# A cross-attention block on one Trainium2 core: TensorE's next value rows moved behind the value sums at hand

## The reference

```python
xn = layer_norm(x, g_norm)
q = xn @ Wq
k, v = jnp.split(context @ Wkv, 2, axis=-1)
q, k, v = map(split_heads, (q, k, v))
k = jnp.concatenate([nk, k], axis=2)
v = jnp.concatenate([nv, v], axis=2)
q = l2norm(q) * q_scale
k = l2norm(k) * k_scale
attn = jax.nn.softmax(jnp.einsum('bhid,bhjd->bhij', q, k) * 8.0, axis=-1)
out = jnp.einsum('bhij,bhjd->bhid', attn, v)
out = out.transpose(0, 2, 1, 3).reshape(b, -1, INNER) @ Wout
return layer_norm(out, g_out)
```

## Time and profile before

| | |
|---|---|
| time, 3 runs | 1354.71, 1362.23, 1365.42 us; median 1362.23 |
| profiled execution | time 1356.67 us, span 1354.6 us, mean granted TensorE clock 0.89 |
| busy | PE 1159.6 us (86%), PEld 746.0, DVE 591.5, ACT 494.3, POOL 439.7 |
| chain that ended last | PE 75%, DVE 10%, issue 9%, ACT 4%, POOL 2% of the span |
| the block of the change | from the first scores at 853.4 us to the last line 1947, which starts at 1267.64 us |

### The profile page before, as it was taken

The page is one execution under the profiler, slowest core; times in us unless marked ns, Lnnn a source line. Parts: engine busy times, 40 slices in busy tenths (PEclk is TensorE's granted clock), DMA queues, the critical chain, the costliest instruction groups (busy, mean ns, idle before and its releaser), DMA issues.

```text
span 1354.6 us, 19075 instructions
## 1 busy us (share of the span) xinstructions
PE 1159.6 (86%) x8054; PEld 746.0 (55%) x8054; DVE 591.5 (44%) x1006; ACT 494.3 (36%) x687; POOL 439.7 (32%) x218
## 2 busy tenths in 40 slices
PE   7999967898787999978775896999999999999358
PEld 4645532365365545544352784677677677677234
DVE  2212357313444632345222514555655655655445
ACT  3344531333132644530332112544345445355011
POOL 0255400000000345500000000577577577577100
PEclk9899968899587999986995796999999999999669
DMA  8333300003000133320013003113113213110100
GB/s 350 140 147 139 129 0 1 0 1 125 0 1 1 74 135 134 140 109 0 0 67 136 1 1 124 64 64 125 63 64 110 79 64 113 68 71 1 68 0 8
DMA packets 23700, 98.77 MB, mean 73 GB/s; under 512 B 2752, under 2 KB 2752, under 8 KB 19904
## 3 DMA queue, kind: packets, MB, share of 16 engines
q1 hardware_dynamic: 23616, 97.56, 18.8%
HBM read 63.74 MB, written 33.82 MB: 72 GB/s over the span
## 4 chain that ended last, share of the span: by engine, by line
PE 75%; DVE 10%; issue 9%; ACT 4%; POOL 2%; DMA 0%; POOLq 0%; DVEq 0%; ACTq 0%
PE PSUM L1865 9%; PE PSUM L1906 9%; PE PSUM L1445 9%; PE PSUM L1926 8%; PE PSUM L1534 3%; PE PSUM L1471 3%; PE PSUM L1454 2%; PE PSUM L1625 2%; PE PSUM L1636 2%; PE PSUM L1489 2%; PE PSUM L1998 1%; DVE ARENA L933 1%; PE PSUM L1822 1%; PE PSUM L1590 1%; PE PSUM L1832 1%
## 5 line engine op out<-in xcount | busy, mean ns | idle before, releaser
L459 POOL TENSOR_TENSOR CK<-CK,ARENA 128x2048 f32<-128x2048 f32 x64 | 290.4, 4537 | 143.4 <-ACT ARENA L703 139.5
L1293 DVE TENSOR_TENSOR ARENA<-PSUM,RK 128x512 f32<-128x512 f32 x256 | 164.1, 683 | 114.7 <-PE PSUM L1906 114.6
L703 ACT ACTIVATE ARENA<-ARENA,WB 128x1024 f32<-128x1024 f32 x128 | 147.0, 1148 | 184.0 <-DVE ARENA L1293 183.9
L397 POOL TENSOR_TENSOR RSTD<-VE,MHALF 128x4 f32<-128x4 f32 x17 | 17.2, 1009 | 473.5 <-DVE VE L769 407.1
L1926 PEld LDWEIGHTS PSUM<-ARENA 128*64 128x64 f32 x2048 | 110.5, 137 | 48.6 <-ACT ARENA L703 43.1
L1906 PE MATMUL PSUM<-ARENA 64*128 64x128 f32 x2048 | 131.8, 278 | 2.7 <-ACT WB L698 2.2
L1445 PE MATMUL PSUM<-CT,WK 128*128 128x512 f32 x256 | 126.9, 622 | 2.4 <-ACT W L483 1.8
L1906 PEld LDWEIGHTS PSUM<-ARENA 64*128 64x128 f32 x2048 | 119.4, 188 | 14.6 <-issue 10.6
L1865 PE MATMUL PSUM<-CK,CT 128*128 128x512 f32 x256 | 126.9, 618 | 0.0
L1926 PE MATMUL PSUM<-ARENA 128*64 128x128 f32 x2048 | 125.9, 276 | 0.4 <-ACT ARENA L703 0.4
L1445 PEld LDWEIGHTS PSUM<-CT,WK 128*128 128x128 f32 x256 | 43.3, 192 | 64.0 <-issue 29.5
(11 more groups left out here) (394 smaller groups left out, 1919.7 us busy)
## 6 DMA issues: line engine op xcount, KB each, us to landing
ARENA<-kept_keys SPq DMA_DIRECT2D x16, 2048.0 KB, 8.3
kept_keys<-KEYS SPq DMA_DIRECT2D x64, 256.0 KB, 2.0
kept_keys<-W SPq DMA_DIRECT2D x64, 256.0 KB, 2.0
CT<-in_ctxT SPq DMA_DIRECT2D x4, 1024.0 KB, 9.9
CK<-in_l0f_experts SPq DMA_DIRECT2D x1, 4096.0 KB, 22.9
CK<-in_ctxk SPq DMA_DIRECT2D x1, 4096.0 KB, 12.7
ARENA<-in_l2f_experts SPq DMA_DIRECT2D x2, 2048.0 KB, 8.2
ARENA<-in_l2f_experts SPq DMA_DIRECT2D x1, 3072.0 KB, 14.0
```

The lines of the kernel that those rows point to most:

```text
L459: nc.gpsimd.tensor_tensor(LS[b % 2], LS[b % 2], PR[:, t % 2, :], ALU.add)\
L703: act(p, p, ACT.Exp, bias=SHIFT).then_inc(sem("l3x_probs"), AC.sends("l3x_probs"))
L1293: ve.tensor_tensor(PR[:, k, q * 512:(q + 1) * 512].rearrange("p (j n) -> p j n", j=4), PSUM[:, 2 + q, :].rearrange("p (j n) -> p j n", j=4 ...
```

## The change

In the loop over tiles TensorE issues the value sums of tile t, and at a batch's first tile the null values in front of them, before the value rows of tile t+1 and not behind them (and behind finish_sums). Nothing else is changed: the same instructions, the same waits, the same order on the other engines.

```diff
                 if t > 1 and t % KEY_TILES == 1:
                     finish_out(t // KEY_TILES - 1)
+                if t % KEY_TILES == 0:
+                    null_values(t // KEY_TILES)
+                values(t)
                 if more:
                     value_rows(t + 1, 0)
                     value_rows(t + 1, 1)
                 if t and t % KEY_TILES == 0:
                     finish_sums(t // KEY_TILES - 1)
-                if t % KEY_TILES == 0:
-                    null_values(t // KEY_TILES)
-                values(t)
             finish_sums(B - 1)
             finish_out(B - 1)
```

## The result

The changed kernel is slower: a median of 1404.97 us (1390.71 to 1410.2) against 1358.47 us for the kernel before, ratio 1.0351 with a 95% interval of 1.0287 to 1.0414. The forecast was 1400 us, in a range of 1376 to 1416. Runs more than 1.5% above the fastest of their kernel count as slow and are left out of the ratios, so a ratio need not be that of the medians given.

The account below looks back on a forecast made before the run. TensorE bounds the kernel between batch ends. Ordinary tiles 21.4, batch ends 17.0, start -1.9 and end +3.8 give +40.3 us: 1397.0 on the profiled scale, 1402.5 on the median's; forecast 1400, range 1376 to 1416.

Parts of the forecast that it names:

- The ordinary tile: Inside a batch: value sums wait 4.28 us after rows, cover only 3.91; tile 6.18 us against 5.797, +0.383 in 56 tiles.
- The batch end: Three batch ends: null values wait for ScalarE's copy, about 6.1 us idle before line 1947; +5.7 us each.
- Start and end: Block's start: null values and V(0) before R(1), -1.9 us; block's end: denominators 4.66 us after V(63), +3.8 us.
- the sum: Whole block: 21.4 + 17.0 - 1.9 + 3.8 = +40.3 us, giving 1397.0 us.
- two scales: Whole time: 1397.0 us from the profiled execution, 1402.5 from the median of the runs; 1400 taken.
- (a): Rival: ordinary tiles pay no wait, only the ends do; 1375.6, some 1378 us between the scales; chance 0.07.
- (c): Rival, every V(t): TensorE passes waiting value sums and starts the rows behind; time stays 1357 to 1362 us; chance 0.05.
- (b): Rival: short pauses in tiles bring the clock down; 1423 us with a tenth of tiles slow, 1530 with half; chance 0.07.
- the stretch of an earlier block: Evidence for no clock loss in tiles: idle in small pieces, 30.84 us busy of 34.00, granted clock 1.00.
- TensorE's busy share inside a batch: Sign inside a batch: TensorE busy for some 94% at a granted clock of 1.00.

Follow-up runs that it names:

- copies-last kernel: Changed kernel, with VectorE copying the first value rows behind quarters 2 and 3, ScalarE the second behind the second exponential: median 1371.36 us, ratio 1.0123.
- the extra copy: One more 128 x 512 VectorE copy per tile before the first value rows' copy: block 491.26 us on the changed kernel, 404.88 on the kernel before.
- The run with 128 rows: Changed kernel with the null-value matmuls over 128 rows of weights in place of one: block 445.76 us, 6.2 less.

## Why the prediction was right, point by point

**The ordinary tile** was right: 6.186 us measured for 6.18, 4.29 us from rows to values for 4.28, and by the measured 0.389 us a tile 56 of them are 21.8 us for 21.4. That it is the copies' place and nothing of TensorE's own is shown by the copies-last kernel (back to 5.797) and the extra copy (+0.6 us a tile after, 0 before). The one row that carried it was the end of the block, where the wait could be seen without cover.

**The batch end** was right in its steps and too small in its size: +7.5 us each in place of +5.7. The null values came 7.09 us after V(15), as worked out; the idle ahead of line 1947 was 6.03 us for 6.1. The missing part is the clock: at the three ends V(16), V(32), V(48) took 3.34, 3.17 and 3.07 us for 1.90, and from R to line 1937 it was 2.94, 3.07 and 3.22 for 2.71, 5.0 us in all. The run with 128 rows takes this part away, and a little of line 1947 with it, and comes out at 445.8, 41.5 over the kernel before, near the forecast's 40.3. Of the remaining 2.4 us most is at line 1947 and the values behind it, where the lower level lasted longer than forecast: line 1947 takes 3.69 us to the next (a granted 0.50) for 3.5, and V(17) to V(18) is 6.59, 6.70 and 6.73 us for 6.18.

**Start and end** were right: V(0) 1.9 us earlier (860.16), 10.84 us from V(62) to line 1937, as in the sum:

```profile
1294.60 1.97 PE L1926 MATMUL PSUM<-ARENA 128*64 128x128 f32 x32
1296.50 1.98 PE L1865 MATMUL PSUM<-CK,CT 128*128 128x512 f32 x4
1300.78 1.97 PE L1926 MATMUL PSUM<-ARENA 128*64 128x128 f32 x32 [2.30 <-ACT ARENA L703]
1305.44 1.94 PE L1937 MATMUL PSUM<-CK,WA 128*64 128x512 f32 x8 [2.69 <-POOL CK L459]
```

**The time** was nearer than the sum. The sum gave 1397.0 us on the scale of the profiled execution, which then took 1404.3, so it was 7.3 us short; that 1400 is within 5 us of the median comes in part from having been set between two scales.

**The rivals.** (a), no cost in ordinary tiles, and (c), rows passing a waiting V, are not seen. (b), that short pauses in every tile bring the clock down, fell as it was put: inside each of the four batches the granted clock is 1.00 with those pauses in each tile; there the swing that the Trainium skill ("TensorE: Matmul & The Clock Gate", section "A second HAM failure mode: psum-queue depth-cycling") tells of another kernel does not arise. That was in part luck: the stretch of an earlier block that the prediction took as evidence does not show idle in many small pieces. Its 3.16 us of idle are two pauses, 0.90 us up to 86.95 and 2.27 us up to 96.67, and TensorE's rows show none between (short ones could lie under the modelled ends); so it is no test of a short pause in every tile. The forecast looked for a clock loss only behind the long idle ahead of line 1947; its sum has none at V(16), where it cost 1.4 us.

**What the profile would show** was wrong in one sign: TensorE's busy share inside a batch did not fall to 94%, it reads 86.30 of 87.00 us, 99%. The pauses are there, but they lie under the modelled ends of the matmuls in front; they show in the weight loads' waits and in the step from row to row.

## What to carry to other kernels

Before moving work on one engine, read the order of its consumers: a step moved back on TensorE is late for every instruction that stands behind its copy on VectorE and ScalarE, ready or not. Work out two sums, the longest way from a result back to the instruction that needs it, and the work that lies between the two in the order of the issuing engine; here the way is 4.28 us, the cover was 5.80 and became 3.91, and the difference is paid in every tile. Where an engine idles at a waiting instruction, look at what stands ready behind it: here putting the values in front, in a kernel that also copies last, took some 9 us off the three batch ends of the kernel before.

## What the runs showed of the hardware

A run of eight matmuls of 512 columns that use one row of weights (1.87 us), behind 0.93 us of idle, was followed at the three ends of the changed kernel by a stretch at a granted 0.50 to 0.60, the lower level for the most part; the same run over 128 rows, behind the same idle, was followed by 1.00. TensorE was busy throughout the run in both. Without that idle just ahead (the kernel before, and the changed kernel with copies last) the run with one row was followed by 1.00 as well. And TensorE's rows read 99% busy here while it lost some 0.4 us in every 6.19.
